# Two products of the triangular merge alternate between quadrants of TensorE, and the plain inverses are stored and loaded before the turned ones

## What is computed

```python
A = -jnp.tril(jnp.einsum('bhncd,bhned->bhnce', kb, k), -1)      # per chunk of 32
T = solve_triangular(eye - A, eye, lower=True)                  # T = (I - A)^-1
u = T @ v
w = T @ kb
def step(S, inp):                                               # 16 chunks in turn
    qi, ki, ui, wi = inp
    attn = jnp.tril(qi @ ki.transpose(0, 1, 3, 2))
    u_i = ui - wi @ S
    o_i = qi @ S + attn @ u_i
    return (S + ki.transpose(0, 1, 3, 2) @ u_i, o_i)
...
x = x + 0.5 * ffn(layernorm(x)); x = x + attn(layernorm(x)); x = x + 0.5 * ffn(layernorm(x))
```

## Time and profile before

| | |
|---|---|
| median of 3 runs | 1264.2 us (1264.02 to 1264.72) |
| span of the profiled execution | 1267.5 us (mean granted TensorE clock 0.918; a time of its own beside the span is not listed) |
| busy share: PE, PEld, DVE, ACT, POOL | 86%, 64%, 66%, 43%, 32% |
| chain that ended last, by engine | PE 55%, DVE 24%, ACT 8%, issue 5%, SP 3%, POOL 3% |
| product rows of the merge, by line | L875 x512, L889 x512, L894 x256, L903 x256, L918 x256 |
| starts of the merges (first L875) | 154.1, 305.8, 444.8, 583.1, 722.1, 865.4, 1005.1, 1142.3 us |

### The profile page before, as it was taken

One profiled execution on the slowest core, in us unless ns is written; L12 is line 12 of the kernel. 1 busy time (PEld: TensorE's weight loads), 2 busy tenths in 40 slices (PEclk: granted clock), 3 DMA queues, 4 the chain that ended last, 5 costly groups with the idle time before them and its releaser, 6 DMA issues.

```text
span 1267.5 us, 25615 instructions
## 1 busy us (share of the span) xinstructions
PE 1090.1 (86%) x10348; PEld 813.0 (64%) x10348; DVE 836.8 (66%) x1556; ACT 547.8 (43%) x957; POOL 410.0 (32%) x640
## 2 busy tenths in 40 slices
PE   3778499789988999889988997899988998887738
PEld 2663387368854886378845894388746885477427
DVE  5754247686678857875677757785687757873363
ACT  1145125543375435643375327443474337531322
POOL 8005500482007610482019500581018400770000
PEclk9869679799999999999999999899999999995768
DMA  5031101402040201402040204101040204010000
GB/s 148 1 80 39 32 1 34 85 1 50 18 92 10 41 9 36 82 1 49 18 100 1 49 2 95 23 18 33 18 101 1 50 1 91 10 31 20 1 0 17
DMA packets 80245, 47.19 MB, mean 37 GB/s; under 512 B 55808, under 2 KB 73728, under 8 KB 80128
## 3 DMA queue, kind: packets, MB, share of 16 engines
q1 hardware_dynamic: 80128, 45.56, 16.0%
HBM read 30.86 MB, written 14.68 MB: 36 GB/s over the span
## 4 chain that ended last, share of the span: by engine, by line
PE 55%; DVE 24%; ACT 8%; issue 5%; SPq 3%; POOL 3%; DMA 1%; DVEq 0%; ACTq 0%; POOLq 0%
PE psum L774 11%; PE psum L776 9%; PE psum L775 9%; DVE conv_acc L1351 5%; PE psum L805 4%; DVE arena L1582 3%; PE psum L963 3%; PE psum L948 2%; PE psum L982 2%; PE psum L987 2%; SPq L346 2%; ACT arena L577 2%; DVE h_hi L1330 2%; PE psum L1140 2%; PE psum L903 2%
## 5 line engine op out<-in xcount | busy, mean ns | idle before, releaser
L515 POOL TENSOR_TENSOR l_prod<-arena 64x30 f32<-64x30 f32 (+14 forms) x240 | 151.5, 631 | 631.3 <-DMA arena<-l_dram 613.1
L573 ACT ACTIVATE h_f<-psum,b_col 128x512 f32<-128x512 f32 x128 | 88.0, 688 | 226.7 <-PE psum L776 205.6
L774 PE MATMUL psum<-w_hi,h_hi 128*128 128x256 f32 x512 | 153.1, 299 | 14.5 <-DVE h_lo L1331 14.4
L519 POOL TENSOR_TENSOR arena<-arena,l_prod 64x30 f32<-64x30 f32 (+14 forms) x240 | 157.2, 655 | 18.8
L776 PE MATMUL psum<-w_hi,h_lo 128*128 128x256 f32 x512 | 146.1, 285 | 0.0
L775 PE MATMUL psum<-w_lo,h_hi 128*128 128x256 f32 x512 | 146.1, 285 | 0.0
L1069 PE MATMUL psum<-v_shift,fir_w 128*32 128x512 f32 x1152 | 136.6, 615 | 3.4 <-DMA v_shift<-v_dram 3.4
L1351 DVE SCALAR_TENSOR_TENSOR conv_acc<-psum,conv_col,conv_acc 128x511 f32<-128x511 f32 x144 | 107.8, 748 | 35.1 <-ACT conv_acc L598 23.3
L1330 DVE CAST h_hi<-h_f 128x512 fp32r<-128x512 f32 x128 | 80.4, 628 | 66.5 <-ACT h_f L573 39.8
L774 PE MATMUL psum<-xt_hi,w_hi 128*128 128x512 f32 x256 | 110.2, 431 | 14.9 <-DVE b_half L1444 7.0
L774 PEld LDWEIGHTS psum<-w_hi,h_hi 128*128 128x128 f32 x512 | 98.9, 193 | 22.5 <-DVE h_lo L1331 18.2
(11 more groups left out here) (231 smaller groups left out, 2268.7 us busy)
## 6 DMA issues: line engine op xcount, KB each, us to landing
x_in<-in_L_attn_x SPq DMA_DIRECT2D x8, 512.0 KB, 4.0
v_dram<-v_fm SPq DMA_DIRECT2D x8, 512.0 KB, 2.8
v_shift<-v_dram SPq DMA_DIRECT2D x8, 512.0 KB, 4.9
out<-x_tok SPq DMA_DIRECT2D x8, 512.0 KB, 2.9
v_shift<-v_dram SPq DMA_DIRECT2D x8, 511.0 KB, 6.9
v_shift<-v_dram SPq DMA_DIRECT2D x8, 510.0 KB, 9.1
v_shift<-v_dram SPq DMA_DIRECT2D x8, 509.0 KB, 11.7
arena<-in_L_ffn_w SPq DMA_DIRECT2D x2, 1024.0 KB, 7.2
```

The lines of the kernel that those rows point to most:

```text
L515: pool.tensor_tensor(prod, l_inv[:, k + 1:, k:k + 1].broadcast_to(shape), l_inv[:, k:k + 1, 0:k].broadcast_to(shape), ALU.mult).then_inc(i ...
L519: pool.tensor_tensor(l_inv[:, k + 1:, 0:k], l_inv[:, k + 1:, 0:k], prod, ALU.add).then_inc(inverted, 1)
L573: act.activation(h_f[:, m % 2, :], bank, ACT.Gelu, bias=b1_col[:, m:m + 1]).then_inc(read, 1)
L774: pe.matmul(dst, a_hi, b_hi, start=first, stop=False, **kw)
```

## The change

- **y2.** The products for the second group of eight units (g = 1) now write output partitions 64 to 127 of their bank, and the two groups alternate instead of following each other. The rows (64 to 127) are the same for both.
- **xab.** The second half of `y_half` and of `t_low` moves to partitions 64 to 127, so that the groups alternate between rows 0 to 63 and 64 to 127, with output partitions 0 to 63 in two banks. PE now waits for both copies of y2 ahead of the first product.
- **t21.** The groups alternate between output partitions 32 to 63 and 96 to 127. ACT copies the result out by two operations of 32x256 instead of one of 32x512.
- **Loads.** Five loads of 32 KB put the plain blocks where these layouts want them, and one of 64 KB fills `t_two` for x12. The zeroing on POOL becomes two memsets, and POOL waits for them ahead of its next operation.
- **Order on SP.** The plain inverses are stored once the diagonal is written, ahead of the turning copy; the turned ones have a semaphore of their own, and the plain loads are issued ahead of the turned ones.

```diff
--- before.py
+++ after.py
@@ -113,10 +113,11 @@
         dv_fm = [v_shift[:, h, 32:WIDE] for h in range(HEADS)]
         c1v = v_shift[:, 0:2, 32:WIDE].rearrange("p g (u d) -> p g u d", d=D)
         l_half = v_shift[D:P, 2:4, 32:WIDE].rearrange("p g (u j) -> p g u j", j=D)
-        y_half = v_shift[0:D, 2:4, 32:WIDE]
+        y_half = [v_shift[0:D, 2, 32:WIDE], v_shift[D:P, 3, 32:WIDE]]
         l_pair = v_shift[:, 4, 32:WIDE].rearrange("p (u j) -> p u j", j=CHUNK)
         y_pair = v_shift[:, 5, 32:WIDE].rearrange("p (u j) -> p u j", j=CHUNK)
         t_low = v_shift[:, 6:8, 32:WIDE].rearrange("p g (u j) -> p g u j", j=D)
+        t_two = v_shift[D:D + CHUNK, 6, 32:WIDE].rearrange("p (u j) -> p u j", j=CHUNK)
         f_fm = sb("f_fm", [P, HEADS, T])
         beta_fm = sb("beta_fm", [32, T])
         rows_tok = sb("rows_tok", [P, 3, UNITS])
@@ -287,7 +288,7 @@
         l_made = sem("l_made")
         l_stored, l_loaded = sem("l_stored"), sem("l_loaded")
         inverted = sem("inverted")
-        t_stored, t_loaded = sem("t_stored"), sem("t_loaded")
+        t_stored, tt_stored, t_loaded = sem("t_stored"), sem("tt_stored"), sem("t_loaded")
         fir_done = sem("fir_done")
         c1v_made = sem("c1v_made")
         t_zeroed = sem("t_zeroed")
@@ -416,19 +417,21 @@
                         sp.dma_start(l_inv[UNITS * c:UNITS * c + UNITS, :, :],
                                      l_dram[c].rearrange("i u j -> u i j")).then_inc(l_loaded, 16)
 
+                    sp.wait_ge(inverted, INV_STEPS * j + INV_STEPS - 1)
+                    sp.dma_start(t_dram.rearrange("c u i j -> (c u) i j"), l_inv[:, :, :]).then_inc(t_stored, 16)
                     sp.wait_ge(inverted, INV_STEPS * j + INV_STEPS)
-                    sp.dma_start(tt_dram.rearrange("c u j i -> (c u) j i"), l_turned[:, :, :]).then_inc(t_stored, 16)
-                    sp.dma_start(t_dram.rearrange("c u i j -> (c u) i j"), l_inv[:, :, :]).then_inc(t_stored, 16)
-                    sp.wait_ge(t_stored, 32 * j + 32)
+                    sp.dma_start(tt_dram.rearrange("c u j i -> (c u) j i"), l_turned[:, :, :]).then_inc(tt_stored, 16)
+                    sp.wait_ge(t_stored, 16 * j + 16)
+                    sp.wait_ge(fir_done, j + 1)
+                    for c, g, row in ((0, 0, 0), (0, 1, 0), (1, 0, 32), (1, 1, D + 32), (0, 1, D)):
+                        col = CHUNK * c
+                        sp.dma_start(t_low[row:row + 32, g, :, col:col + CHUNK],
+                                     t_dram[c, 8 * g:8 * g + 8].rearrange("u i j -> i u j")).then_inc(t_loaded, 16)
+                    sp.dma_start(t_two, t_dram[2].rearrange("u i j -> i u j")).then_inc(t_loaded, 16)
+                    sp.wait_ge(tt_stored, 16 * j + 16)
                     for c in range(CPT):
                         sp.dma_start(x_t[32 * c:32 * c + 32, :, 32 * c:32 * c + 32],
                                      tt_dram[c].rearrange("u j i -> j u i")).then_inc(t_loaded, 16)
-                    sp.wait_ge(fir_done, j + 1)
-                    for c in range(CPT - 1):
-                        col = CHUNK * (c % 2)
-                        for g in range(2):
-                            sp.dma_start(t_low[32 * c:32 * c + 32, g, :, col:col + CHUNK],
-                                         t_dram[c, 8 * g:8 * g + 8].rearrange("u i j -> i u j")).then_inc(t_loaded, 16)
                 if at.back:
                     i = at.i
                     sp.wait_ge(y_made, 2 * i + 2)
@@ -532,7 +535,9 @@
 
                     pool.wait_ge(fir_done, j + 1)
                     pool.sem_inc(passed, 1)
-                    pool.memset(t_low[0:CHUNK, :, :, CHUNK:D], 0.0).then_inc(t_zeroed, 1)
+                    for g in range(2):
+                        pool.memset(t_low[D * g:D * g + CHUNK, g, :, CHUNK:D], 0.0).then_inc(t_zeroed, 1)
+                    pool.wait_ge(t_zeroed, 2 * j + 2)
                 if at.back:
                     pool.wait_ge(xn_made[2], 2 * at.i + 2)
                     for t in range(TILES):
@@ -639,9 +644,12 @@
                     front_gelu(2)
                     out_of(at, "y1", 0, y_pair[0:32, :, :], src=lambda b: pairs(b[0:32, :]))
                     out_of(at, "x12", 0, x_t[0:32, :, 32:64], src=lambda b: pairs(b[0:32, :]))
-                    out_of(at, "t21", 0, t_low[32:64, :, :, 0:CHUNK],
-                           src=lambda b: b[32:64, :].rearrange("p (g u j) -> p g u j", g=2, j=CHUNK))
-                    out_of(at, "y2", 1, y_half[:, 1, :], src=lambda b: b[0:D, :])
+                    bank, read = arrive(act, at, "t21")
+                    for g in range(2):
+                        rows = slice(D * g + 32, D * g + 64)
+                        last = act.activation(t_low[rows, g, :, 0:CHUNK], pairs(bank[rows, 256 * g:256 * g + 256]), ACT.Copy)
+                    last.then_inc(read, 1)
+                    out_of(at, "y2", 1, y_half[1], src=lambda b: b[D:P, :])
                     front_gelu(3)
                     out_of(at, "xab", 0, x_t[0:D, 0:UNITS // 2, D:P], src=lambda b: b[0:D, :].rearrange("p (u j) -> p u j", j=D))
                     stat_square(at, 0)
@@ -886,39 +894,43 @@
                 for u in range(UNITS):
                     for q in (1, 0):
                         rows = slice(D * q, D * q + 32)
-                        last = pe.matmul(banks[q][0][rows, 32 * u:32 * u + 32], t_low[rows, u // 8, u % 8, 0:CHUNK],
-                                         y_pair[rows, u, :], start=True, stop=True)
+                        t_of = t_two[:, u, :] if q else t_low[rows, u // 8, u % 8, 0:CHUNK]
+                        last = pe.matmul(banks[q][0][rows, 32 * u:32 * u + 32], t_of, y_pair[rows, u, :], start=True, stop=True)
                         if u == UNITS - 1:
                             last.then_inc(banks[q][1], 1)
-                for u in range(UNITS):
-                    last = pe.matmul(t_bank[32:64, 32 * u:32 * u + 32], y_pair[0:32, u, :], t_low[0:32, u // 8, u % 8, 0:CHUNK],
-                                     start=True, stop=True)
+                for n in range(UNITS // 2):
+                    for g in range(2):
+                        u = 8 * g + n
+                        last = pe.matmul(t_bank[D * g + 32:D * g + 64, 32 * u:32 * u + 32], y_pair[0:32, u, :],
+                                         t_low[0:32, g, n, 0:CHUNK], start=True, stop=True)
                 last.then_inc(t_full, 1)
                 fill(at, range(8, 10))
 
                 copied(pe, at, "x12", 1)
                 banks = [claim(pe, at, "y2", b) for b in range(2)]
                 pe.sem_inc(passed, 1)
-                for u in range(UNITS):
-                    last = pe.matmul(banks[u // 8][0][0:D, D * (u % 8):D * (u % 8) + D], l_half[:, u // 8, u % 8, :], x_t[D:P, u, D:P],
-                                     start=True, stop=True)
-                    if u % 8 == 7:
-                        last.then_inc(banks[u // 8][1], 1)
+                for n in range(UNITS // 2):
+                    for g in range(2):
+                        last = pe.matmul(banks[g][0][D * g:D * g + D, D * n:D * n + D], l_half[:, g, n, :],
+                                         x_t[D:P, 8 * g + n, D:P], start=True, stop=True)
+                        if n == UNITS // 2 - 1:
+                            last.then_inc(banks[g][1], 1)
                 fill(at, range(10, 12))
 
                 copied(pe, at, "t21")
                 copied(pe, at, "x12", 0)
                 pe.wait_ge(c1v_made, i + 1)
-                pe.wait_ge(t_zeroed, i + 1)
+                pe.wait_ge(t_zeroed, 2 * i + 2)
                 banks = [claim(pe, at, "xab", b) for b in range(2)]
-                for u in range(UNITS):
-                    if u % 8 == 0:
-                        copied(pe, at, "y2", u // 8)
-                        pe.sem_inc(passed, 1)
-                    last = pe.matmul(banks[u // 8][0][0:D, D * (u % 8):D * (u % 8) + D], t_low[0:D, u // 8, u % 8, :],
-                                     y_half[:, u // 8, D * (u % 8):D * (u % 8) + D], start=True, stop=True)
-                    if u % 8 == 7:
-                        last.then_inc(banks[u // 8][1], 1)
+                copied(pe, at, "y2", 0)
+                copied(pe, at, "y2", 1)
+                pe.sem_inc(passed, 1)
+                for n in range(UNITS // 2):
+                    for g in range(2):
+                        last = pe.matmul(banks[g][0][0:D, D * n:D * n + D], t_low[D * g:D * g + D, g, n, :],
+                                         y_half[g][:, D * n:D * n + D], start=True, stop=True)
+                        if n == UNITS // 2 - 1:
+                            last.then_inc(banks[g][1], 1)
                 fill(at, range(12, 14))
                 copied(pe, at, "xab", 0)
                 copied(pe, at, "xab", 1)
@@ -1409,7 +1421,7 @@
                     dve.tensor_copy(x_t[64:96, :, 96:128], bank[64:96, :].rearrange("p (u j) -> p u j", j=CHUNK)).then_inc(read, 1)
```

(2 more changed lines are left out.)

## The result

The changed kernel took 1227.6 us as the median of four runs (1222.8 to 1230.0), the kernel before 1264.1 as that of its four: ratio 0.973, 95% interval 0.969 to 0.976. Six more runs of it gave 1226.7 (experiment 5), so that all ten have a median of 1227.0. The forecast was 1239.7 us and its range began at 1231: the direction was right, and the forecast gain too small, 24.5 us where some 36 were measured. Its profiled execution took 1227.4 us and spans 1225.7.

A forecast was written before the change was run, and what follows sets the result against it. PE was taken as the bound in merges 1 to 6, with waits for loads at merges 0 and 7. Terms 14.2 + 2.4 + 3.0 + 1.5 + 2.6 + 0.8 = 24.5 us off 1264.2 gave 1239.7 us, range 1231 to 1250.

The forecast's parts named there:

- Steady merges: Merges 1 to 6: alternating y2, xab and t21 products save 2.37 us a merge, 14.2 us over six.
- Merge 0, products: First merge: shorter t21, y2 and xab save 2.4 us, the saving at full rate, although the clock was at half.
- Merge 0, loads: Ahead of the first merge: earlier plain store and loads save 3.0 us of PE's wait.
- Merge 7, loads: Last merge: loads come 3 us earlier, but DVE's residual addition then holds the first product, so 1.5 us saved.
- Merge 7, products: Last merge: shorter products bring L948 2.6 us nearer, with 0.8 us for the joint wait on y2's copies included.
- POOL and DVE: End of the inversion: POOL's wait behind the zeroing lets a held h_lo in earlier; 0.8 us, bounds 0 and 1.6.
- The gap between merges: Stretch from one merge to the next: the forecast sum had no saving for it.
- same rows, no overlap: Rival, 8%: alternating output partitions alone give y2 and t21 no overlap, only xab gains; 12.1 us saved, 1252.1 us.
- Given back later in the pass: Rival, 13%: DVE or ACT holds PE later in a pass, half of the 14.2 us is lost; 1246.8 us.
- The clock helps at both ends: Rival, 10%: the clock stays at 2.4 GHz longer around merges 0 and 7, 8 us more saved; 1231.7 us.
- The clock falls in steady merges: Rival, 4%: granted clock falls to 0.50 in steady merges, 10.9 us lost each; 1305.1 us with all six.

The follow-up runs named there:

- experiment 5: The changed kernel again with no edit, for a second profile: 1226.7 us, ratio 0.9708.
- run 6: The kernel before with only the new order of stores and loads (plain inverses stored ahead of the turning copy, t_low's loads first): 1255.2 us, ratio 0.9937.
- run 4: The changed kernel with the old order of stores and loads (both stores behind the turning copy, x_t's loads first): 1234.2 us, ratio 0.9773.
- run 12: The changed kernel with t21, y2 and xab products in turn instead of alternating, repeated for a second profile: 1253.0 us.
- run 13: The kernel before with the new order of stores and loads and POOL's wait behind the zeroing, products as they were: 1251.5 us, ratio 0.9914.
- run 7: The changed kernel with y2 and t21 products in turn and xab still alternating: 1241.3 us, ratio 0.9817.
- run 10: The kernel before with POOL waiting between the turning copy and the zeroing, and not between zeroing and bias additions: 1261.5 us, ratio 0.9987.

## Why the prediction was wrong, and where it was right

The step that failed is the path at the end of a pass and into merge 7. I had DVE's residual hold merge 7's first product, and I gave the new wait on GpSimd only 0.8 us; the runs show that this wait removes the hold that made the residual late, so that the loads stay last there, and that both together are worth 6.3 us and not 2.3. The products and the loads ahead of merge 0 came as summed. Of the 36 us measured a further 7.8 stand in no term and are not explained.

- *Steady merges, 14.2:* right. 6 x 2.35 = 14.1 us. Of it the alternation gives 1.92 a merge and the split layout, which I had not priced, 0.43; I had the sum right, and its split wrong.
- *Merge 0, products, 2.4:* right as a product term, too small as a change of the mean. With an early clock merge 0 takes 15.4 to 16.0 us in turn and 12.9 to 13.6 alternating: 2.4 on the means. But I read the 17.2 us of half clock in the earlier trace rows as part of the kernel. It is a draw: with all or some of the products in turn, the clock was back 4.5 to 5.8 us after the restart in eight of eleven profiles and 10.5 to 17.2 us after in three. With all alternating it was back after 4.3 to 5.9 us in five of five. If the late draw is really gone, that is 1 to 2 us more on the mean; five profiles don't show it.
- *Merge 0, loads, 3.0:* right, 3.0.
- *Merge 7, loads, 1.5:* the wrong path. I held y1 back to the end of DVE's residual at the place it had in the earlier trace rows. That place followed from a cast that had been held for 4.65 us at the end of the inversion; the new wait took the hold away, the residual now starts 8.0 instead of 10.6 us behind the copy's start, and the loads stayed last: 2.8 us, and 0.7 more in the merge behind it, with the clock. I had priced the two edits apart where the one uncovers the other. Even with a cast held for 4.61 us, in run 6, it was 2.1.
- *Merge 7, products, 2.6:* about right, 2.3. In the old order of loads the merge takes 13.8 us in five of the six profiles with the old products, and 11.48 with the new (run 4).
- *POOL and DVE, 0.8 (0 to 1.6):* too small. I counted only the passes in which h_lo was held and PE was seen to wait for it. All holds of 3 us and more are gone, casts too, and the wait alone is worth 2.8 us (0.9 to 4.8).
- *The gap between merges, 0:* the sum of gaps 1, 2, 3 and 5 (gap n follows merge n; gaps 0 and 6 lie beside merges 0 and 7, and gap 4 has the draw of some 7 us named at run 12) is 500.0 us on the mean of four profiles without the wait (498.5 to 501.9; run 6, with the new order alone, has 499.7), 499.3 with the wait alone or with the order (three, 498.9 to 499.7), and 497.3 in the eight with the new layout (495.4 to 499.1), whatever the order of their products. The first 0.7 would be the wait's, within the spread. The other 2.0 arise mostly ahead of the copy, between 53 and 82 us behind the recurrence's start, and no experiment shows their cause.

Taken together: order 3.0 + 2.8 + 0.7, wait 2.8, products 14.1 + 2.4 + 2.3, which is 28.1 us, against 35.9 between the medians of all runs. Most of the shortfall lies with the products: the medians of run 13 and of the changed kernel's ten runs are 24.5 us apart (the means 25.5, with a 95% interval of 22 to 29), and the rows give 18.8. The clock of merge 0 (1 to 2) and the gaps (2.0 over four of the seven) would fill over half of that in size, but for the one there are too few draws and for the other there is no cause.

The clocks of the single runs point to where the rest lies. Each run has a mean granted clock, and from it comes the time at half clock, as twice (1 - mean) of the span. It is 190 us on the mean of the 74 runs of before beside the experiments, and 166 in the changed kernel's ten. Among runs of one kernel every us less at half clock goes with 0.32 us less time (173 runs in twelve sets, 0.29 to 0.35; run 13 is left out, because its profiled run has 0.95 on record where the others have 1.00, at unchanged row times), and most of the 3.9 us of spread goes with it (correlation 0.85 in the 74 runs). By that slope the 24 us would be worth 7.6 us, an estimate that overlaps with the terms at merges 0 and 7. No run sets the clock, so this is shown as going together and not as a cause, and why the changed kernel draws fewer slow stretches stays open.

Of the rivals, *same rows, no overlap* is refuted by run 7, and with it, for these products, the rule that stood against the change (Trainium skill, TensorE: Matmul & The Clock Gate, Part 3, "The mechanism"): the rows of y2 start 30 ns apart on the mean ((1.15 - 0.22) / 31) when their output partitions alternate, and 58 to 59 when they don't, and t21 gains likewise in its one bank. *Given back later in the pass* did not happen; the gaps got shorter. *The clock helps at both ends* had the right side: merge 7 gets 1.6 us at full clock, and the runs spend 24 us less at half clock. The window that it was priced from did not change: 0.50. *The clock falls in steady merges* did not happen, 1.00 in the window. The other rule, that a DVE operation with two SBUF inputs contends only with a GpSimd operation that reads SBUF (Trainium skill, SBUF — State Buffer, "Who interferes with whom"), would have let h_lo run beside the zeroing, which reads nothing. In run 10 an h_lo arrives 0.14 us behind the start of the zeroing, needs 0.69 us where nothing holds it, and ends 3.73 us later, behind the additions. By that rule the term was 0; the wait measured 2.8 us.
